# Value products of a causal and two full attentions: 512 query columns in every second slot, with the jobs in those slots

## The reference, cut to what matters

```
x = x + attn(layernorm(x))            # 16 heads of 16, rotary embedding, full softmax over 512 keys
h = layernorm(x)
y = softmax(causal(q k^T)) v          # 16 heads, queries see earlier keys only
y = y + softmax(qc kc^T) vc           # the same queries' tokens against the context, full
x = x + y @ Wp + bp
x = x + moe(layernorm(x))             # 16 experts, one per token, at most 256 tokens each, relu
```

## Time and profile before

| what | value |
|---|---|
| median of 3 runs | 1626.52 us |
| the profiled execution, from the first to the last instruction | 1626.3 us |
| PE busy | 1443.6 us, 89% |
| DVE busy | 1204.3 us, 74% |
| ACT busy | 1062.0 us, 65% |
| mean granted TensorE clock | 0.963 of full |

### The profile page before, as it was taken

How to read it: one execution, slowest core, us unless ns; L and a number is a source line. 1 busy time by engine, 2 the same in 40 slices (tenths; PEclk the granted TensorE clock), 3 DMA queues, 4 the chain that set the end, 5 groups by cost and what they waited for, 6 DMA issues and landing times.

```text
span 1626.3 us, 37857 instructions
## 1 busy us (share of the span) xinstructions
PE 1443.6 (89%) x14610; PEld 647.8 (40%) x14610; DVE 1204.3 (74%) x2434; ACT 1062.0 (65%) x2139; POOL 650.5 (40%) x535
## 2 busy tenths in 40 slices
PE   3799999999999898898998989989989978779997
PEld 1222322333333433334334244333343432359997
DVE  6788878888876776776877877768778677537774
ACT  2377777778777676676676676766766656425662
POOL 2544565466422422236145333352352211225554
PEclk8699999999999999999999999999999999889999
DMA  6435344444323433323323322332333211157771
GB/s 179 115 119 141 105 112 115 120 115 112 92 60 95 110 88 101 90 83 104 82 83 88 104 80 69 96 98 71 85 100 97 60 45 39 48 189 262 251 259 62
DMA packets 119479, 175.82 MB, mean 108 GB/s; under 512 B 26273, under 2 KB 85895, under 8 KB 114696
## 3 DMA queue, kind: packets, MB, share of 16 engines
q1 hardware_dynamic: 111376, 158.50, 34.4%
q0 software_dynamic: 5888, 14.24, 2.7%
q10 hardware_dynamic: 2048, 0.83, 0.2%
HBM read 102.33 MB, written 51.18 MB: 94 GB/s over the span
## 4 chain that ended last, share of the span: by engine, by line
PE 54%; DVE 17%; DMA 9%; ACT 6%; issue 6%; POOL 5%; SPq 2%; POOLq 0%; DVEq 0%; ACTq 0%
PE psO L741 13%; PE psM L466 9%; PE psS L764 9%; DVE negmax L1193 9%; PE psK L466 6%; PE psK L795 6%; PE psS L466 4%; ACT probs L1029 4%; DMA recipB<-recip_scratch 3%; PE psK L693 2%; DVE xn L1165 2%; DMA shared<-shared 1%; DVE stats L1141 1%; DMA stack<-mrows 1%; PE psM L831 1%
## 5 line engine op out<-in xcount | busy, mean ns | idle before, releaser
L1193 DVE TENSOR_REDUCE negmax<-psS 128x1 f32<-128x512 f32 (+3 forms) x1536 | 869.4, 615 | 273.6 <-PE psS L764 136.4
L1029 ACT ACTIVATE probs<-psK 128x512 f32<-128x512 f32 (+3 forms) x1536 | 753.7, 544 | 325.3 <-PE psK L795 198.4
L741 PE MATMUL psO<-probs,V 128*32 128x256 f32 (+1 forms) x5632 | 446.1, 389 | 23.8 <-ACT U L1021 17.8
L764 PE MATMUL psS<-stack 48*128 48x512 f16 (+3 forms) x1536 | 284.5, 367 | 57.2 <-DVE negmax L1193 53.7
L795 PE MATMUL psK<-stack 50*128 50x512 f16 (+3 forms) x1536 | 278.5, 359 | 26.1 <-DMA stack<-mrows 14.7
L764 PEld LDWEIGHTS psS<-stack 48*128 48x128 f16 x1536 | 74.2, 93 | 373.2 <-DVE negmax L1193 290.7
L741 PEld LDWEIGHTS psO<-probs,V 128*32 128x32 f32 x5632 | 113.5, 109 | 210.9 <-issue 122.8
L1427 POOL TENSOR_TENSOR rstd<-lnt,minus_half 128x4 f32<-128x4 f32 x24 | 24.7, 1028 | 193.1 <-DVE lnt L1157 193.1
L795 PEld LDWEIGHTS psK<-stack 50*128 50x128 f16 x1536 | 76.5, 95 | 57.4 <-ACT probs L1029 23.6
L1553 POOL DMA_INDIRECT out_dram<-stack,put_to x32 | 76.8, 2399 | 17.8 <-issue 9.1
L1441 POOL CAST shared<-shared 128x512 f16<-128x512 f32 x8 | 4.9, 612 | 191.2 <-ACT shared L1051 191.2
(11 more groups left out here) (192 smaller groups left out, 2063.1 us busy)
## 6 DMA issues: line engine op xcount, KB each, us to landing
spare<-in_L_ffn_w_dram SPq DMA_DIRECT2D x32, 1024.0 KB, 6.3
parts_scratch<-parts SPq DMA_DIRECT2D x192, 128.0 KB
stack<-parts_scratch SPq DMA_DIRECT2D x96, 256.0 KB, 4.0
stack<-parts_scratch SPq DMA_DIRECT2D x96, 128.0 KB, 4.2
packed<-U SPq DMA_DIRECT2D x192, 64.0 KB
recipB<-recip_scratch SPq DMA_DIRECT2D x48, 256.0 KB
shared<-shared SPq DMA_DIRECT2D x48, 128.0 KB, 2.1
probs<-back_scratch POOLq DMA_DIRECT2D x16, 258.0 KB, 3.1
```

What stands on the lines that cost most here:

```text
L741: mm = nc.tensor.matmul(psO[32 * i:32 * i + 32, q0:q1], v_of(par)[:, kt, 2 * g + i % 2 + PAIRS * (i // 2), :], probs[:, (unit + i % 2) % P ...
L764: mm = nc.tensor.matmul(psS[:, banks[hh], 0:n], stack_of(par, 0)[rows, hp, qt * P:(qt + 1) * P], stack_of(par, 1)[rows, hp, 0:n], start=Tr ...
L1029: nc.scalar.activation(probs[:, t % P_RING, i, q0:T], psK[:, S_BANKS[t][i], q0:T], ACT.Exp, scale=SM_SCALE / (1 if b.kind == "A" else WSCA ...
L1193: nc.vector.tensor_reduce(negmax[:, g % 2, at:at + 1], psS[:, S_BANKS[u // 2][j], 0:n], AX_X, ALU.max, negate=True).then_inc(s["max_done"], 1)
```

## The change: what it does

1. `Body.av`: value products stand in odd slots alone, with all query columns of the unit (512, in kind B 512, 384, 256 or 128) in one matmul per head.
2. `evacuated`: the copy of psO to U stands in the slots 1, 9, 17, 25, behind the last value product of a group and two slots before the next group's first. SyncE's DMAs from U stay in their slots (2, 16, 24, 30).
3. `SLOTS_OF` of AA, AB, AC, BB and CC: every job stands in one slot, an odd one (but for zT1, out0 and out1 of CC); no job is cut over two or three slots any more. Splits, stores and normalisation move by a slot or two with them.
4. Unread matmuls: `WARM_END` is gone; `WARM_JOB` has two each in the slots 5 and 7 of A and B, and 13 and 25 of C. Before there were 156 of them over the 24 bodies, now 96.

```diff
-    "AA": {"v0": (1, 2), "v1": (3, 4), "xT0": (7,), "xT1": (8,), "proj0": (12,), "proj1": (15,), "proj2": (18, 20),
-           "proj3": (22, 23), "out0": (25,), "out1": (26, 27), "ln": (1, 3, 4, 6), "load": (2, 3, 6, 7, 8, 9, 10, 11),
+    "AA": {"v0": (1,), "v1": (3,), "xT0": (7,), "xT1": (9,), "proj0": (11,), "proj1": (15,), "proj2": (19,),
+           "proj3": (23,), "out0": (25,), "out1": (27,), "ln": (1, 3, 4, 6), "load": (2, 3, 6, 7, 8, 9, 10, 11),
...
-WARM_JOB = {"A": {5: 2, 7: 2}, "C": {25: 2}}
-WARM_END = {"AA": {6: 2}, "AB": {6: 2, 7: 2}, "BB": {6: 2, 7: 2, 30: 2}, "CC": {12: 3, 15: 2}}
+WARM_JOB = {"A": {5: 2, 7: 2}, "B": {5: 2, 7: 2}, "C": {13: 2, 25: 2}}
...
         kind = self.kind if t >= 3 else self.prev
-        if not kind:
+        if not kind or t % 2 == 0:
             return None
-        half = (t + 1) % 2
-        unit = (t - 3 - half) % SLOTS
-        first = q_from(kind, unit % 8 // 2)
-        q0, q1 = max(first, half * T // 2), (half + 1) * T // 2
-        return (t < 3, unit, q0, q1, q0 == first) if q0 < q1 else None
+        unit = (t - 3) % SLOTS
+        return t < 3, unit, q_from(kind, unit % 8 // 2)
...
-            if t == 2 and b.prev:
+            if t == 1 and b.prev:
                 return NG - 1
-            return t // 8 - 1 if b.kind and t > 2 and t % 8 == 2 else None
+            return t // 8 - 1 if b.kind and t > 1 and t % 8 == 1 else None
...
-                    ago = {2: 0, 16: 6, 24: 6, 30: 4}.get(t)
+                    ago = {2: 1, 16: 7, 24: 7, 30: 5}.get(t)
...
-                            mm = nc.tensor.matmul(psO[32 * i:32 * i + 32, q0:q1], v_of(par)[:, kt, 2 * g + i % 2 + PAIRS * (i // 2), :],
-                                                  probs[:, (unit + i % 2) % P_RING, i // 2, q0:q1],
-                                                  start=kt == 0 and q0 == 0, stop=kt == TT - 1, skip_group_check=True)
+                            mm = nc.tensor.matmul(psO[32 * i:32 * i + 32, q0:T], v_of(par)[:, kt, 2 * g + i % 2 + PAIRS * (i // 2), :],
+                                                  probs[:, (unit + i % 2) % P_RING, i // 2, q0:T],
+                                                  start=kt == 0, stop=kt == TT - 1, skip_group_check=True)
```

More of the change, by code:

```diff
@@ L65 @@
                "ln": (2, 3, 4, 5), "lower": (14, 16, 30, 31), "store": (16, 30, 31, 31)},
-    "AA": {"v0": (1, 2), "v1": (3, 4), "xT0": (7,), "xT1": (8,), "proj0": (12,), "proj1": (15,), "proj2": (18, 20),
-           "proj3": (22, 23), "out0": (25,), "out1": (26, 27), "ln": (1, 3, 4, 6), "load": (2, 3, 6, 7, 8, 9, 10, 11),
[L68 to L77, removed]
+    "AA": {"v0": (1,), "v1": (3,), "xT0": (7,), "xT1": (9,), "proj0": (11,), "proj1": (15,), "proj2": (19,),
+           "proj3": (23,), "out0": (25,), "out1": (27,), "ln": (1, 3, 4, 6), "load": (2, 3, 6, 7, 8, 9, 10, 11),
+           "split": (8, 10), "lower": (18, 22, 26, 30), "store": (20, 23, 30, 31), "recip": 7, "norm": 13, "attn": 15, "bias": 1},
@@ new lines @@
+    "AB": {"v0": (1,), "v1": (3,), "xT0": (7,), "xT1": (9,), "proj0": (15,), "proj1": (17,), "proj2": (19,), "proj3": (23,),
+           "out0": (25,), "out1": (31,), "ln": (2, 3, 5, 6), "load": (1, 2, 3, 5, 6, 8, 9, 10),
+           "split": (8, 10, 16, 18, 20, 24), "store": (18, 20, 22, 26), "recip": 5, "norm": 12, "attn": 20, "bias": 1},
+    "AC": {"v0": (1,), "v1": (3,), "ctxT0": (7,), "proj0": (9,), "proj1": (11,), "proj2": (15,), "proj3": (17,),
+           "out0": (23,), "out1": (31,), "load": (1, 3, 3, 6, 7, 9, 9, 10), "split": (8, 10, 12, 16, 18),
+           "store": (12, 14, 18, 20), "recip": 8, "norm": 13, "attn": 15, "bias": 0},
@@ L729, in _ @@
                     if av:
-                        prev, unit, q0, q1, first = av
+                        prev, unit, q0 = av
                         par = np_ if prev else b.parity
                         g, kt = unit // 8, unit % 8 // 2
[L733 to L738, removed]
+                        need(pe, s["exp_done"], b.at("exp_done", 0 if prev else 2 * unit + 4))
+                        if not prev and unit == 0:
+                            pe.wait_ge(s["v_out"], b.at("v_out"))
+                        if kt == 0:
+                            need(pe, s["av_out"], b.at("av_out", int(b.prev is not None) + g))
                         for i in range(GH):
-                            mm = nc.tensor.matmul(psO[32 * i:32 * i + 32, q0:q1], v_of(par)[:, kt, 2 * g + i % 2 + PAIRS * (i // 2), :],
-                                                  probs[:, (unit + i % 2) % P_RING, i // 2, q0:q1],
-                                                  start=kt == 0 and q0 == 0, stop=kt == TT - 1, skip_group_check=True)
+                            mm = nc.tensor.matmul(psO[32 * i:32 * i + 32, q0:T], v_of(par)[:, kt, 2 * g + i % 2 + PAIRS * (i // 2), :],
+                                                  probs[:, (unit + i % 2) % P_RING, i // 2, q0:T],
+                                                  start=kt == 0, stop=kt == TT - 1, skip_group_check=True)
                         mm.then_inc(s["av_done"], 1)
@@ L813, in _ @@
                     if t in b.warm_job:
-                        keep_warm(spare_bank(b, t), b.warm_job[t])
+                        need(pe, s["exp_done"], b.at("exp_done", 2 * t))
+                        keep_warm(psK[:, 3 - sum(S_BANKS[t]), :], b.warm_job[t])
                     for idx, (slot, name, j, first) in enumerate(jobs):
```

17 lines of the change are left out of this document (7 added, 10 removed).

## The result

| | before | after |
|---|---|---|
| median of 4 runs | 1626.54 us | 1683.95 us |
| lowest and highest | 1622.08 to 1627.76 | 1675.26 to 1690.82 |
| profiled execution, span | 1626.3 us | 1683.0 us |
| mean granted TensorE clock | 0.963 | 0.932 |

The account below looks back on a forecast made before the run. No engine alone was taken as the bound: PE in slots with a job, DVE narrowly in others, the reciprocals' chain in B. Gains of 17 (A), 17 (C) and 12 (B), 46 less 8, took 1626.3 to 1588 us; range 1556 to 1640.

Parts of the forecast that it names:

- 3072 records: Sign that value products fell from 704 to 384; joining 320 pairs at 0.23 us saves PE 74 us.
- light pair: Two neighbouring slots without a large job: 2.8 us together, where two light slots took 2.4 before.
- The wait for U: Value products waiting for the copy of psO, 17.8 us in all before, were to wait no longer.
- A5's slots 1 to 8: Stretch of a kind A body, 14.6 us forecast: DVE's 14.0 us stay, plus 0.6 of starting gaps.
- its slots 17 to 0: Second part of a B body: 26.3 to 24.7 us, gain 1.6, for 8 bodies 12 us.
- Rival 3: Slower, at value products behind odd slots: late ACT makes light pairs 3.1 us; 1648 us in all, chance 0.16.
- I take 8 us off: Deduction from the gain: three more half-clock stretches of 1.5 us each, and 3.5 us of added waits for transfers.
- the promise: In B, the chain from reciprocals to slot 16's exponentials stays 13 to 14 us, with PE's longer wait before slot 17.
- rival 4: The clock: one more half-clock stretch in every body, 1620 us; sign, mean clock 0.94 or less; chance 0.08.
- The 46 us: Sum of gains before the deduction: 17 us in kind A, 17 in C, 12 in B.
- Rival 2: DVE, ACT and the reciprocals' chain keep the bodies as long as they are: 1622 us, chance 0.14.

Follow-up runs that it names:

- e5: Changed kernel with AA normalisation back in slot 12, BB's second split in 11, AA store in 22, attention casts in 17 (AA) and 18 (BB): 1603.92 us, ratio 0.9859.
- e1: Changed kernel with the normalisation of AA in slot 12 in place of 13, ahead of proj0's rotary products on POOL: 1652.79 us, ratio 1.0146.
- e2: Changed kernel with the second split of BB in slot 11 in place of 12, ahead of the normalisation products on POOL: 1659.32 us, ratio 1.0205.
- e7: Changed kernel with 32 unread matmuls behind slot 15's job in AA, filling PE's wait there: 1677.8 us, ratio 1.0296.
- e12: e11 with two more unread matmuls each in slots 6, 8 and 10 of kind B: 1606.77 us, ratio 0.9849 to the kernel before.
- e11: e5 with the third step of the routing's layer norm in CC in slot 14 in place of 13: 1598.34 us, ratio 0.9821 to the kernel before.
- e8: Kernel before with the normalisation of AA in slot 14 in place of 13, behind proj0's rotary products on POOL: 1665.13 us, ratio 1.0222.

## Why the prediction was wrong

*Right.* Line 730 has 3072 records. The 512-column product steps 1.0 us (408.55 to 409.54 in A5). The light pair is 2.83 us, 2.8 forecast. The wait for U is gone. A5's slots 1 to 8 take 14.16 us (14.6). C17 gained 2.6 (2.2), partly since it has no half clock now, where its second half in the earlier trace rows stood at 0.94. Half right is B: its slots 17 to 0 gained 0.8 us in the changed kernel (1.6). Rival 3, which had the loss, had the wrong place: it wanted light pairs of 3.1 us.

*Wrong: the moves of the table at almost nothing.* The step that failed is in the sum: "I take 8 us off: three more such stretches, and 3.5 us of added waits", where the waits were "for transfers that PE doesn't reach today". The added waits and what they draw after them were some 80 us: so much is off with both orders put back and the casts and a store moved (e5), and 31 and 25 of it with e1 and e2 alone. And they were in the main not transfers that PE had come closer to, but work on POOL that had changed places. The text followed PE and ACT through the table's moves and cited POOL's chain only as something that doesn't get shorter. It did not ask what now stands ahead of it. In B the promise was 13 to 14 us from the reciprocals to slot 16's exponentials; it is 19.1 (1019.73 to 1038.87), and the wait is in front of slot 15's job, not of slot 17.

*Wrong in part: the clock.* Mean clock 0.932 is what rival 4 named (0.94 or less), but it goes with the waits. (1 - 0.932) x 1683 x 2 = 229 us at half clock, an estimate, against 120 before by the same sum. The Trainium skill (TensorE: Matmul & The Clock Gate, § Why this matters for your kernels) says that long idle gaps between bursts are what lets the clock go; here the trace agrees for the new waits, since the clock falls at each of the twelve of 3.8 to 8.9 us in A1 to A5 and B8 to B20, and e7 shows it at 1.00 with the gap filled. Long gaps aren't the whole of it: in B16 of e5 it falls at 956.7 us behind 6.7 us in which PE is busy 4.8 and waits 1.2 us at the longest. e7 also bounds the clock's share: a third of the loss of A5.

*The 46 us, once the waits are gone.* From slot 0 to slot 0, in us, all at a granted clock of 1.00 but C17 before (0.97):

| body | before | forecast | best seen |
|---|---|---|---|
| A5 | 55.4 | 53.3 | 54.9 (e12) |
| B16 | 52.3 | 50.7 | 50.55 (e11) |
| C17 | 56.2 | 54.0 | 53.2 (e1) |

These are the best bodies, not the mean ones. The sizes of B and C were reached, that of A was not: 0.5 us of 2.1. For B the place was wrong: of B16's 1.8 us in e11 slots 17 to 0 have 0.6 (26.3 to 25.7), where all of it was forecast, and slots 1 to 16 have 1.1 (25.4 to 24.3), where none was. In A5 slots 1 to 8 gained 1.0, but slots 9 to 0 take 40.9 us in e5 (371.81 to 412.70), where the pairs of the forecast add up to 38.7. Job and supply stand too close there: PE still waits 0.87 us in front of slot 11's job, two slots behind the transposes that feed it through ACT and POOL, and 0.65 in front of the exponentials' products of slot 18. e12's profiled execution, the fastest of its six and with no half clock in B and C, is 49 us below the profiled one of the kernel before. That is the size of the forecast sum of 46, with A at 8 in place of 17, and B and C at 20 each in place of 12 and 17. A part of these two comes from half clock that the kernel before has and this execution has not, so the agreement is in part luck.

*Rival 2* had 1622 us. Its rule was that of the Trainium skill (Perfetto Trace Analysis, § Identifying the Most-Contended Engine), which sets weight loads, beside the share of the peak arithmetic, in place of busy matmuls. By it DVE would be the bound, since weight loads are 40% of the span. That is not borne out: DVE's busy time is the same in all versions (1199 to 1205 us), and the profiled spans go from 1577 to 1684.

## What to carry to other kernels

When a table of slots moves a job, write down for every engine the queue in which its followers stand, the "quiet" ones too, and look for two neighbours that changed places. A short piece of work that waits for a DMA, put in front of a long one that others wait for, makes them wait for the DMA too: in A5 of e8 that is 7.18 us of PE's time, from one number. And judge a regular layout only after its new waits have been taken out, since some 80 us of slips hid a gain of 23 to 30.

## What the runs showed of the hardware

- Behind a wait of 7.75 us came 7 us and more of work at half clock. The stretch behind it:

```profile
422.45:429.47 7.02, 6.67 (x28) 0.97 (x30) 2.58 (x4) 5.25 (x10) 5.85 (x5) 0.50 0.33 114
```

PE is busy 6.67 of 7.02 us there, at a granted clock of 0.50, the 1.2 GHz level.
- The swap DMA of 128 KB took 6.32 us in A5, and 4.42 in the kernel before, while the page has 2.0 and 2.1 us as the medians of this form. Loads of recipB and of stack, up to 256 KB each, were issued ahead of it on the same queue within the 6 us before (403.26 to 406.43, the swap at 408.87); that they are what held it up was not tested. A median of landings doesn't price the one that matters.
- Executions of one program on one chip differ by over 2%: e12 from 1579 us at a mean clock of 0.978 to 1616 at 0.958. The clock doesn't tell the whole: two between them took 1595 at 0.968 and 1606 at 0.969.
